# Normalising four tiles at a time, channel by channel, in an audio kernel's layer norm

## The reference

```
h = dct(frames(x))                       # 32 x 938 x 128
n = layernorm(h)                         # over the 128 channels of a frame
h = h + causal_convolution_along_frames(n, kernel from nu, theta, gamma)
h = h + moe(layernorm(h))                # 8 experts pick 1024 frames each, 128->512->128
```

## Time and profile before

| | |
|---|---|
| Median of 3 runs (lowest, highest) | 683.19 us (680.26, 684.93) |
| The profiled execution: device time; span from first to last instruction | 681.69 us; 679.9 us |
| Mean granted TensorE clock | 0.817 of full speed |
| Busy share of the span: PE, DVE, ACT, POOL | 60%, 69%, 41%, 44% |
| L1094 (statistics), 512 instructions | 105.1 us busy on DVE |
| L1124 (the operation that is changed), 128 instructions | 54.9 us busy on DVE, 545 ns mean |
| L1516 (power -1/2 for the front stage), 16 instructions | 46.9 us busy on POOL, 2930 ns mean |

### The profile page before, as it was taken

The page is one execution under the profiler, slowest core; times in us unless marked ns, Lnnn a source line. Parts: engine busy times, 40 slices in busy tenths (PEclk is TensorE's granted clock), DMA queues, the critical chain, the costliest instruction groups (busy, mean ns, idle before and its releaser), DMA issues.

```text
span 679.9 us, 11771 instructions
## 1 busy us (share of the span) xinstructions
PE 406.7 (60%) x3465; PEld 324.0 (48%) x3465; DVE 468.1 (69%) x1771; ACT 280.8 (41%) x530; POOL 298.7 (44%) x207
## 2 busy tenths in 40 slices
PE   3878577887887568777500001332689666966910
PEld 3867477744776557754300000221366554755710
DVE  6799876799399977588888888889963455345210
ACT  3777510155577630035464453000474632554400
POOL 1466600065366630035400000577777865566474
PEclk9999788989889979999855555555699779977965
DMA  7699239898368606799699700011234443333232
GB/s 145 120 254 240 50 79 180 201 259 222 75 107 151 125 8 156 184 283 245 213 306 348 252 1 0 25 48 50 51 82 58 43 58 57 60 33 54 17 30 23
DMA packets 87291, 83.23 MB, mean 122 GB/s; under 512 B 8843, under 2 KB 84107, under 8 KB 86987
## 3 DMA queue, kind: packets, MB, share of 16 engines
q1 hardware_dynamic: 75706, 58.86, 36.3%
q0 software_dynamic: 11264, 8.40, 9.7%
q10 hardware_dynamic: 272, 15.37, 6.8%
HBM read 58.09 MB, written 39.39 MB: 143 GB/s over the span
## 4 chain that ended last, share of the span: by engine, by line
issue 32%; DVE 27%; PE 20%; POOL 13%; ACT 3%; DMA 2%; DVEq 1%; SPq 1%; POOLq 0%; ACTq 0%
PE banks L994 9%; POOL small L1516 6%; PE banks L981 5%; POOL small L1537 4%; DVE stats L1094 3%; POOL out L1559 3%; DVE xn L1124 2%; PE banks L783 2%; DVE xn L1278 2%; DVE xn L1400 1%; PE banks L968 1%; DVE xn L1336 1%; DVE place L1388 1%; DVE xin L1382 1%; DMA xin<-in_x 1%
## 5 line engine op out<-in xcount | busy, mean ns | idle before, releaser
L1559 POOL DMA_INDIRECT out<-hid,index x64 | 100.6, 1572 | 54.4 <-DVE hid L1461 34.5
L1547 POOL DMA_INDIRECT hid<-kept,index x64 | 66.5, 1040 | 115.4 <-issue 115.1
L1094 DVE BATCH_NORM_STATS2 stats<-hid 120x6 f32 (+1 forms) x512 | 105.1, 277 | 9.7 <-ACT hid L602 8.4
L1537 POOL TENSOR_TENSOR small<-small,powers 120x16 f32<-120x16 f32 x16 | 46.4, 2900 | 119.1 <-DVE small L1118 119.1
L682 ACT ACTIVATE xt<-banks 128x480 f32<-128x480 f32 x64 | 36.4, 572 | 115.2 <-PE banks L868 115.2
L783 PE MATMUL banks<-const,xt 128*120 128x128 f32 x512 | 73.0, 290 | 16.2 <-ACT xt L597 16.2
L848 PE MATMUL banks<-xn,ring 122*120 122x128 f32 x512 | 67.7, 292 | 19.3 <-DMA ring<-answers 8.5
L783 PEld LDWEIGHTS banks<-const,xt 128*120 128x120 f32 x512 | 64.3, 193 | 22.5 <-ACT xt L597 14.3
L848 PEld LDWEIGHTS banks<-xn,ring 122*120 122x120 f32 x512 | 63.5, 202 | 23.6 <-DMA ring<-answers 14.1
L1516 POOL TENSOR_TENSOR small<-small,powers 120x16 f32<-120x16 f32 x16 | 46.9, 2930 | 51.2 <-DVE small L1118 51.2
L994 PE MATMUL banks<-w_ring,xn 128*128 128x128 f32 x512 | 67.8, 298 | 0.0
(11 more groups left out here) (199 smaller groups left out, 727.7 us busy)
## 6 DMA issues: line engine op xcount, KB each, us to landing
ring<-toeplitz SPq DMA_DIRECT2D x128, 120.0 KB
kept<-out ACTq DMA_DIRECT2D x1, 15008.0 KB, 50.8
xin<-in_x SPq DMA_DIRECT2D x28, 480.0 KB, 7.0
out<-hid SPq DMA_DIRECT2D x14, 960.0 KB, 10.6
w_ring<-in_L_ffn_W SPq DMA_DIRECT2D x16, 256.0 KB, 3.0
toeplitz<-ring SPq DMA_DIRECT2D x6, 545.0 KB, 11.1
out<-hid SPq DMA_DIRECT2D x2, 784.0 KB
xin<-in_x SPq DMA_DIRECT2D x4, 384.0 KB
```

The source lines that it names most:

```text
L1094: ins = dve.bn_stats(stats[:, slot, b, :], hid[:, bass.ds(c * HB + b, 1), :].rearrange("p a k -> p (a k)"))
L1537: pool.tensor_tensor(small[:, slot, 4, :], small[:, slot, 2, :], powers[0:L, :], ALU.pow).then_inc(rstd2_ready, 1)
L1547: pool.indirect_dma_start(found[:, n, :], None, kept, bass.IndirectOffsetOnAxis(ap=index[:, n:n + 1], axis=0)).then_inc(found_in[e], 16)
L1559: pool.indirect_dma_start(rows, bass.IndirectOffsetOnAxis(ap=index[:, n:n + 1], axis=0), adds[:, n, :], None, compute_op=ALU.add, oob_is_e ...
```

## The change

`normalise` on VectorE no longer issues one `tensor_scalar` a tile ((hid - mean) * scale, both factors one value a partition). It covers four tiles at once with two `tensor_tensor` operations over 4 x 128 words: `xn <- hid * scale`, then `xn <- xn + shift`, where scale and shift are rows 4 and 6 of `small`, repeated over the channels. The order of the elements is channel by channel, the four tiles innermost: so the writes and the second read of `xn` take 4 neighbouring words at a time, and the read of `hid` steps 128 words from every element to the next. The second operation waits for the first, and a wait for `bias` (`nb_ready`) is added, since row 6 is now read. The tiles 0 to 3 are done in one piece behind the statistics of group 2, instead of in two pieces ahead of it and behind it. At the end of a half the eight tiles are one piece, two operations over 1024 words.

```diff
                 def normalise(c, slot, first, last):
-                    for b in range(first, last):
-                        ins = dve.tensor_scalar(xn[0:L, :, bass.ds(c * HB + b, 1)].rearrange("p k a -> p (k a)"),
-                                                hid[:, bass.ds(c * HB + b, 1), :].rearrange("p a k -> p (a k)"),
-                                                small[:, slot, 5, b:b + 1], small[:, slot, 4, b:b + 1],
-                                                ALU.subtract, ALU.mult)
+                    tiles = bass.ds(c * HB + first, last - first)
+                    rows = xn[0:L, :, tiles]
+                    scale, shift = (small[:, slot, n, first:last].unsqueeze(1).broadcast_to([L, D, last - first])
+                                    for n in (4, 6))
+                    dve.tensor_tensor(rows, hid[:, tiles, :].rearrange("p b k -> p k b"), scale,
+                                      ALU.mult).then_inc(dve_own, own.one())
+                    dve.wait_ge(dve_own, own.all())
+                    ins = dve.tensor_tensor(rows, rows, shift, ALU.add)
                     if last == DVE_TILES:
                         ins.then_inc(xn_dve, 1)
...
                         if n == 1 and not first:
                             bias(c - 1, 1 - slot)
-                        if n in (1, 2) and not first:
-                            normalise(c - 1, 1 - slot, 2 * n - 2, 2 * n)
+                            dve.wait_ge(nb_ready, c + CHUNKS * h)
+                        if n == 2 and not first:
+                            normalise(c - 1, 1 - slot, 0, DVE_TILES // 2)
...
                         moments(slot, var_ready)
-                        normalise(c - 1, 1 - slot, 4, DVE_TILES)
+                        normalise(c - 1, 1 - slot, DVE_TILES // 2, DVE_TILES)
...
-                for cc in own.loop(1, CHUNKS // 2 - 1, 14):
+                for cc in own.loop(1, CHUNKS // 2 - 1, 18):
...
                 bias(CHUNKS - 1, 1)
+                dve.wait_ge(nb_ready, CHUNKS * (h + 1))
                 normalise(CHUNKS - 1, 1, 0, DVE_TILES)
```

## The result

The changed kernel takes 703.92 us in the median of 4 runs (700.35 to 709.94), the kernel before 684.06 (4 runs, 680.26 to 687.39): a ratio of 1.030, with a 95% interval of 1.0205 to 1.0397. The forecast was 705 us, slower. The profiled execution has a span of 704.4 us where the one before had 679.9.

What follows compares the result with a forecast made beforehand. Bound: front-stage ring of GpSimd's power, VectorE's tiles and statistics, and moments. Turns (14.6 to 21.3 us) plus halves' ends (1.7 to 3.2) gave 16.3 to 24.5, taken as 22; 681.7 + 22 + 1.5 gave 705 us, range 684 to 718.

Steps and rivals of the forecast that it cites:

- Exclusion between GpSimd and a `tensor_tensor` with two SBUF inputs: Front stage: the two wait for each other's on-chip memory access; forecast with a read near 1.1 us, 696 to 712, chance 0.65.
- one 0.11 us case and a rule: Setup: GpSimd's L1502 takes 0.30 us beside two-input L1082, otherwise 0.19; the skill says a port pair is held exclusively.
- The first operation, 1.10 us: The 512-word read of hid in 128-word steps: 0.69 us plus 0.81 ns an element, taken from L1434.
- the rival of dear reads: Exclusion, but the first operation takes 1.5 us or more: 718 us at 1.5, 740 at 2.2; chance 0.10.
- Tiles 0 to 3, +0.77 us a turn: From bias to group 3's statistics: GpSimd's L1525 takes over between the two operations, and the second pays 0.80 us.
- The power, +0.27 or +0.75: Tiles 4 to 7 behind the moments: +0.27 us after using 0.47 slack, or +0.75 if GpSimd's power waits for the first operation.
- the upper branch: GpSimd's power read waits for the first operation of tiles 4 to 7: +0.75 us, making 1.52 us a turn.
- the row against it: GpSimd's power L1516 takes 2.93 us with short L1124 tiles around it, 2.90 with none, so short ones do not delay it.
- 14 turns, 14.6 to 21.3 us: Front-stage chunks of both halves: 1.04 to 1.52 us more in each of 14 turns.
- A half's end, +0.85 to +1.6 us each: Two operations over 1024 words delay the state work by 0.85 us, 1.6 with the power's 0.75; twice, 1.7 to 3.2.
- no exclusion (688 us): GpSimd and tensor_tensor do not block each other, first operation 1.10 us: +4.6 us in all; chance 0.15.
- the faster case: No exclusion and the strided read free (0.69 us): tiles 0 to 3 gain 0.44 a turn, -5.8 us, 677 us; chance 0.10.

Runs made afterwards that it cites:

- e1: Changed kernel with VectorE's scale and shift factors copied to PSUM, so tensor_tensor has one SBUF input except at a half's end; 697.34 us, ratio 1.0216 to the kernel before.
- e7: Changed kernel, but GpSimd does two operations over 4 words and a memset instead of normalising its four tiles; one run, 709.4 us against 708.6 for the kernel before.
- e2: Changed kernel, but the first operation reads hid in memory order instead of 128-word steps (values land in wrong places); 691.44 us, ratio 1.0138 to the kernel before.
- e4: Changed kernel, but tiles 4 to 7 go back to one tensor_scalar a tile; 692.03 us, ratio 1.0143 to the kernel before.
- e3: Kernel before with its one-tile tensor_scalar operations, in the changed kernel's order and with its wait for bias; 685.85 us, ratio 1.0059.
- e6: Changed kernel with both four-tile pieces behind the moments, clear of GpSimd's two normalising operations; ratio 1.0255 to the kernel before.
- e1b: As e1, but the 8-word operation making the shift factor reads 1/std from its PSUM copy; ratio 1.0126 to the kernel before.
- e8: Kernel before with its tensor_scalar operations, all eight tiles behind the moments and bias behind group 0's statistics; 678.38 us against 682.50, ratio 0.9944.

## Why the prediction was right

**Exclusion between GpSimd and a `tensor_tensor` with two SBUF inputs**: shown. It was taken on the strength of one 0.11 us case and a rule. `e1` takes the pair away, and in the first turn of each half leaves the rest in its place; `e7` takes GpSimd's reading away.

**The first operation, 1.10 us**: measured 1.04 (27 of the 28 over 512 words take 1.02 to 1.07 us). So the rival of dear reads, 1.5 us or more, falls. The row chosen for it, L1434 with its 8-word steps, gave 0.81 ns more a word; a 128-word step costs 0.70 (`e2`). That they are so near is in part luck: L1434 also sums its result (`accum_out`), and no row or run parts that from its steps. The Trainium skill's page "Vector Engine (DVE) Microarchitecture Reference", section "Measured stream behaviour on trn2", has 1.73 ns a column for one source that hops 4 KiB at every element. The prediction's estimate from it, 1.04 us, was nearer, though the step here is 512 bytes.

**Tiles 0 to 3, +0.77 us a turn**: measured +0.60. The stall was taken as 0.80 from a tile issued 0.09 us behind L1525; here L1530 had been waiting for L1127's end, and the second operation pays 0.68. The rest is the shorter first operation. In one turn the order is the other way round, a natural control. The timeline of the second half:

```profile
212.58 1.08 POOL L1530 TENSOR_TENSOR xn<-between,small 120x512 f32 x1 [0.18 <-POOL between L1527]
212.65 1.80 DVE L1127 TENSOR_TENSOR xn<-hid,small 120x512 f32 x1 [0.17 <-issue]
214.49 0.69 DVE L1130 TENSOR_TENSOR xn<-xn,small 120x512 f32 x1
```

L1127 starts 1.45 us behind bias, 0.25 later than in the loop's other turns, and so behind L1530: it pays 0.76 us and L1130 nothing.

**The power, +0.27 or +0.75**: measured 3.56 to 3.69 us in every turn, so about +0.7; only a half's first power, with no L1127 ahead of it, keeps 2.9. So the upper branch was right, and the row against it, L1516 unmoved beside L1124's tiles, only said that operations of 0.26 us apiece are short enough. `e4` shows both in one kernel.

**14 turns, 14.6 to 21.3 us**: 19.9. Outside the loop a turn costs 1.27 more, in it 1.54. In the loop the wait for bias, which the prediction counted as outside it (0.03 us), holds VectorE 0.24 us in each of 8 turns, and the power grows by 0.72 instead of 0.66. So the branch that turned out right said 1.52 and the mean is 1.42, but in part by cancellation: tiles 0 to 3 were taken 0.17 too dear, and the loop's longer wait was missing. The changed kernel's waits (who waited for whom, us in total, times, longest):

```profile
DVE stats L1094 <- DVE small L1137: 1.9, 8, 0.2
```

**A half's end, +0.85 to +1.6 us each**: +0.53 (bias to the first state operation, 90.87 to 96.04, before 80.81 to 85.45) and +0.44. The two operations over 1024 words take 2.78 and 1.89 us instead of the 2.90 and 2.02 of the sum. And the upper figure was wrong by its own working: the power ahead of the last bias lies in the seventh turn and had been counted there already. So this term was mis-sized. The upper branch, which held throughout, adds up to 24.5 us; the sum took 22 between the branches, and the medians say 19.9, the traces 20.9 with both ends. That 705 us came so near is partly this hedge.

**The rivals**: no exclusion (688 us) falls with `e1` and `e7`, the faster case with them; the order by itself is at most a fifth of the loss (`e3`). What each removal gave back in the turns: the stride 8 us (`e2`), the long operations behind the moments 10 (`e4`), GpSimd's reading 10 (`e7`, 120.0 us for 14 turns). These are not shares of the loss: `e2` and `e4` overlap in the power's wait, and what `e7` removes is a stall that the kernel before has in the same place too.

## What to carry to other kernels

A VectorE operation with two SBUF inputs, or in the form of L1124, ran one after the other with GpSimd operations that read SBUF, so before small operations are merged into long ones, look at what GpSimd issues beside them and which of the two is on the critical ring. A factor in PSUM takes the stall away (`e1`), and so does a place where GpSimd computes rather than reads (`e6`), but neither was enough here: both kernels stayed slower than the one before, as another wait took over. Issue small operations for which others wait ahead of GpSimd's next read: in `e1b` bias, 16 words, decided between turns of some 8.2 and 9.2 us. The only run faster than the kernel before (`e8`, 0.6%) kept the small operations and changed their place.

## What the runs showed that was not expected

- An operation of 8 or 16 words stalls as long as one of 512: it takes 0.96 us (`e1`) and 1.04 (`e1b`) instead of 0.17, and a few hundredths of a microsecond in the order of issue decide on it.
- A GpSimd power of 2.9 us over 16 words lets VectorE's short operations through all along, but waits for a long one that began before it (3.56 to 3.69 us behind 1.04, 3.27 to 3.37 behind 0.69). This fits an instruction that reads briefly and then computes; its reading was not seen by itself.
- `tensor_tensor` with one input from PSUM costs the same as an unblocked one with two from SBUF: 1.02 to 1.07 us with the stride, 0.69 without it (`e1`).
